# A vision-tower block on one core: the long convolution at its start, rebuilt in its tables, its products and its place beside the weight preparation

## The reference, cut to what matters

```python
dt = jnp.exp(log_dt)
A = -jnp.exp(inv_A_real) + 1j * A_imag
dtA = A * dt[:, None]
dA = (1.0 + dtA / 2) / (1.0 - dtA / 2)
V = jnp.exp(jnp.log(dA)[:, :, None] * jnp.arange(L))     # powers dA**l, l = 0 to 255
K = 2.0 * jnp.einsum('chn,hnl->chl', C * B[None], V).real # C is x
```

## Time and profile before

| what | value |
|---|---|
| median of 3 runs | 591.04 us (590.71 to 592.91) |
| profiled execution | 593.25 us, span 591.4 us |
| PE busy | 452.1 us, 76% |
| DVE busy | 379.4 us, 64% |
| ACT busy | 272.2 us, 46% |
| POOL busy | 188.3 us, 32% |
| mean granted clock of TensorE | 0.947 |
| powers, to the last square on DVE | 0 to 27.8 us |
| tables, to POOL's last | to 51.3 us |
| chunks, first product to last sum | 54.6 to 125.9 us |
| first statistics of a group | 133.5 us |

### The profile page before, as it was taken

One profiled execution on the slowest core, in us unless ns is written; L12 is line 12 of the kernel. 1 busy time (PEld: TensorE's weight loads), 2 busy tenths in 40 slices (PEclk: granted clock), 3 DMA queues, 4 the chain that ended last, 5 costly groups with the idle time before them and its releaser, 6 DMA issues. The chain is left out here.

```text
span 591.4 us, 11267 instructions
## 1 busy us (share of the span) xinstructions
PE 452.1 (76%) x3664; PEld 403.6 (68%) x3664; DVE 379.4 (64%) x895; ACT 272.2 (46%) x544; POOL 188.3 (32%) x156
## 2 busy tenths in 40 slices
PE   0000665584998999879999999998999999989645
PEld 0000654473776778668898898897988988989544
DVE  4999997766677665625466658557566485563632
ACT  1101342432776766454666545744565446544310
POOL 0197784722111210105070520703406107031200
PEclk9999999695999999969999999999999999999966
DMA  4100458953112202000010200201102001010101
GB/s 108 35 1 1 124 142 242 270 153 115 37 37 72 99 35 72 35 15 24 1 37 1 71 0 0 71 0 39 32 0 71 0 0 35 0 37 1 35 0 37
DMA packets 37816, 30.86 MB, mean 52 GB/s; under 512 B 19488, under 2 KB 31136, under 8 KB 37792
## 3 DMA queue, kind: packets, MB, share of 16 engines
q1 hardware_dynamic: 18848, 22.17, 12.1%
q10 hardware_dynamic: 18944, 8.39, 5.0%
HBM read 17.97 MB, written 12.58 MB: 52 GB/s over the span
## 5 line engine op out<-in xcount | busy, mean ns | idle before, releaser
L1109 PE MATMUL PS<-prods,Wa 128*64 128x64 f32 x512 | 37.7, 243 | 85.8 <-DVE prods L796 58.2
L978 DVE TENSOR_TENSOR gl<-PS,gh 128x512 fp32r<-128x512 f32 x64 | 44.2, 690 | 78.3 <-ACT gh L618 51.6
L1109 PEld LDWEIGHTS PS<-prods,Wa 128*64 128x64 f32 x512 | 32.2, 147 | 89.9 <-DVE prods L796 58.1
L615 ACT ACTIVATE PS<-PS,fc1bias 128x512 f32<-128x512 f32 x64 | 42.0, 657 | 94.8 <-PE PS L266 94.7
L264 PE MATMUL PS<-fc2h,gh 128*128 128x256 f32 x256 | 74.4, 291 | 6.0 <-DVE gl L978 5.2
L266 PE MATMUL PS<-fc2l,gh 128*128 128x256 f32 x256 | 72.3, 283 | 0.0
L265 PE MATMUL PS<-fc2h,gl 128*128 128x256 f32 x256 | 72.3, 282 | 0.0
L437 POOL TENSOR_SCALAR pst<-mv 128x4 f32<-128x4 f32 x16 | 3.6, 228 | 207.9 <-DVE pst L962 207.9
L264 PEld LDWEIGHTS PS<-fc2h,gh 128*128 128x128 f32 x256 | 48.6, 190 | 10.7 <-DVE gl L978 6.0
L264 PE MATMUL PS<-x2Th,fc1h 128*128 (+1 forms) x128 | 52.4, 409 | 2.1 <-DVE x2Tl L949 2.1
L265 PE MATMUL PS<-x2Th,fc1l 128*128 (+1 forms) x128 | 50.9, 398 | 0.0
(11 more groups left out here) (179 smaller groups left out, 1354.5 us busy)
## 6 DMA issues: line engine op xcount, KB each, us to landing
h_scratch<-tokev ACTq DMA_DIRECT2D x16, 256.0 KB, 3.0
h<-h_scratch SPq DMA_DIRECT2D x16, 256.0 KB, 5.0
q_scratch<-qe ACTq DMA_DIRECT2D x16, 256.0 KB, 2.1
qf<-q_scratch SPq DMA_DIRECT2D x16, 256.0 KB, 2.9
out_tokens<-outb SPq DMA_DIRECT2D x16, 256.0 KB, 2.2
...
craw<-in_c_ri SPq DMA_DIRECT2D x32, 64.0 KB, 2.4
...
```

The source lines that it names most:

```text
L615: act.activation(bank(j % 2), bank(j % 2), ACT.Gelu, bias=fc1bias[:, j:j + 1]).then_inc(gact, 1)
L978: dve.tensor_tensor(gl[:, j % 2, :], bank(j % 2), gh[:, j % 2, :].bitcast(F32), ALU.subtract).then_inc(gldone, 1)
L1109: mm = pe.matmul(dst, w[:, par, s * SUB + i, :, :].rearrange("p c d -> p (c d)"), prods[:, s, 0, i, :], start=x == 0, stop=x == 1)
```

## The change

It rebuilds the convolution in five places.

1. **Powers.** The squares move to ACT (`Square`). A level keeps two operations on DVE: the imaginary part, and the real part as twice the square of the real part minus the squared modulus; ACT squares the modulus as well. The three loads that the exponentials need go first, and ACT issues the two loads of `aim` itself. The first entries of `X` and `Y` are made by ACT too.
2. **Tables.** `Er`, `Ei` have seven entries (e = 1 to 7; EX). ACT copies entries 1, 2 and 4 of them; POOL makes entry 3, the third entry of `U`, and entries 5 to 7 in one rotation of three (18 operations after the powers). ACT makes the signed entries of `U`.
3. **Products.** A chunk is no longer cut in halves: DVE makes two products and a sum of 16 x 8 x 7 = 896 columns into `M`, which has a buffer for each parity; ACT copies `X` as the entry e = 0. PE runs all 32 matmuls of a chunk in one group, and ACT takes the result in one copy of 512 columns.
4. **Weights.** SP issues all weight loads right behind the first two chunks' c, and PE multiplies them before the token matmuls, while the tables are made. DVE's addition to `fc1bias`, which needs them, stands ahead of its first product.
5. **Loads of h0.** The first half goes out one or two loads at a time between the loads of c for chunks 12 to 15.

```diff
-SUB = 8
+EX = NE - 1
...
-            sp.dma_start(ldt[:, :], logdt.unsqueeze(0).to_broadcast([P, H])).then_inc(ld_tab, 16)
-            for r in range(2):
-                rows = slice(r * N, (r + 1) * N)
-                sp.dma_start(iar[rows, :], inv_ar).then_inc(ld_tab, 16)
-                sp.dma_start(aim[rows, :], a_im).then_inc(ld_tab, 16)
-                sp.dma_start(btab[rows, 0, :], b_ri[r]).then_inc(ld_tab, 16)
-                sp.dma_start(btab[rows, 1, :], b_ri[1 - r]).then_inc(ld_tab, 16)
+            halves = [slice(r * N, (r + 1) * N) for r in range(2)]
+            sp.dma_start(ldt[:, :], logdt.unsqueeze(0).to_broadcast([P, H])).then_inc(ld_exp, 16)
+            for rows in halves:
+                sp.dma_start(iar[rows, :], inv_ar).then_inc(ld_exp, 16)
+            for r, rows in enumerate(halves):
+                sp.dma_start(btab[rows, 0, :], b_ri[r]).then_inc(ld_b, 16)
+                sp.dma_start(btab[rows, 1, :], b_ri[1 - r]).then_inc(ld_b, 16)
...
-            with sp.Fori(0, PAIRS // 2 + 1) as it:
-                for par in range(2):
-                    load_c(it, par)
-            load_c(PAIRS // 2 + 1, 0)
-            load_h0(0)
-            load_c(PAIRS // 2 + 1, 1)
-            sp.wait_ge(dve_set, DVE_TABLES)
-            sp.wait_ge(pool_set, POOL_TABLES)
+            for par in range(2):
+                load_c(0, par)
+            sp.wait_ge(pool_set, 1)
             load_weight(routraw[:, :, 0:LEAVES - 1], routersT)
-            load_weight(wqraw[:, :, :], wq)
-            load_c(PAIRS // 2 + 2, 0)
-            load_weight(leafraw[:, :, :], leafT)
-            load_weight(woutraw[:, :, :], woutT)
-            load_c(PAIRS // 2 + 2, 1)
-            load_weight(fc1raw[:, :, :], fc1T)
-            load_c(PAIRS // 2 + 3, 0)
-            load_weight(projraw[:, :, :], projT)
-            load_c(PAIRS // 2 + 3, 1)
-            load_weight(fc2raw[:, :, :], fc2T)
-            load_h0(1)
+            for dst, src in ((wqraw, wq), (leafraw, leafT), (woutraw, woutT), (fc1raw, fc1T), (projraw, projT),
+                             (fc2raw, fc2T)):
+                load_weight(dst[:, :, :], src)
+            for n in range(2, CHUNKS - 5):
+                load_c(n // 2, n % 2)
+            load_c((CHUNKS - 5) // 2, (CHUNKS - 5) % 2)
+            for par in range(2):
+                sp.wait_ge(h0st[par], CREDIT + 16 * (PAIRS // 2))
+            load_h0(0, 0)
+            load_c((CHUNKS - 4) // 2, (CHUNKS - 4) % 2)
+            load_h0(0, 1)
+            load_h0(0, 2)
+            load_c((CHUNKS - 3) // 2, (CHUNKS - 3) % 2)
+            load_h0(0, 3)
+            load_h0(0, 4)
+            load_c((CHUNKS - 2) // 2, (CHUNKS - 2) % 2)
+            load_h0(0, 5)
+            load_h0(0, 6)
+            load_c((CHUNKS - 1) // 2, (CHUNKS - 1) % 2)
+            load_h0(0, 7)
+            for par in range(2):
+                sp.wait_ge(h0st[par], CREDIT + 16 * PAIRS)
+            for g in range(GROUPS):
+                load_h0(1, g)
...
-            link(pool.memset(Er[:, :, 0], 1.0))
-            link(pool.memset(Ei[:, :, 0], 0.0))
+            link(pool.memset(routraw[:, :, LEAVES - 1:LEAVES], 0.0))
+
+            def rotated(outr, outi, ar, ai, br, bi, t):
+                link(pool.tensor_tensor(outr, ar, br, ALU.mult))
+                link(pool.tensor_tensor(t, ai, bi, ALU.mult))
+                link(pool.tensor_tensor(outr, outr, t, ALU.subtract))
+                link(pool.tensor_tensor(outi, ar, bi, ALU.mult))
+                link(pool.tensor_tensor(t, ai, br, ALU.mult))
+                link(pool.tensor_tensor(outi, outi, t, ALU.add))
+
             pool.wait_ge(dve_set, DVE_POWERS)
...
+            rotated(Er[:, :, 2], Ei[:, :, 2], pw[:, 0, 0, :], pw[:, 0, 1, :], pw[:, 1, 0, :], pw[:, 1, 1, :],
+                    tE[:, :, 0])
+            rotated(U[:, 0, 2, :], ui[:, 2, :], U[:, 0, 0, :], ui[:, 0, :], U[:, 0, 1, :], ui[:, 1, :], tE[:, :, 0])
+            pool.wait_ge(e_out, 6)
+            wr, wi = (pw[:, 2, x, :].unsqueeze(2).to_broadcast([P, H, 3]) for x in range(2))
+            rotated(Er[:, :, 4:7], Ei[:, :, 4:7], Er[:, :, 0:3], Ei[:, :, 0:3], wr, wi, tE[:, :, :])
...
-            act.wait_ge(ld_tab, 16 * 9)
+            for r in range(2):
+                act.dma_start(aim[r * N:(r + 1) * N, :], a_im).then_inc(ld_aim, 16)
+            zi, omz, t0, den, m = (base[:, k, :] for k in (3, 4, 5, 6, 9))
+            act.wait_ge(ld_exp, 16 * 3)
             act.activation(base[:, 0, :], ldt[:, :], ACT.Exp).then_inc(act_tab, 1)
             act.activation(base[:, 1, :], iar[:, :], ACT.Exp).then_inc(act_tab, 1)
+            act.wait_ge(dve_set, 9)
+            act.activation(t0, zi, ACT.Square).then_inc(act_tab, 1)
+            act.wait_ge(dve_set, 10)
+            act.activation(den, omz, ACT.Square).then_inc(act_tab, 1)
+            act.wait_ge(ld_b, 16 * 4)
+            act.activation(X[:, :, 0], btab[:, 0, :], ACT.Copy, scale=sgn[:, 1:2]).then_inc(b_out, 1)
+            act.activation(Y[:, :, 0], btab[:, 1, :], ACT.Copy, scale=-2.0).then_inc(b_out, 1)
+            act.wait_ge(dve_set, DVE_Z)
+            act.activation(PS[:, 0, 0:H], pw[:, 0, 0, :], ACT.Square).then_inc(act_tab, 1)
+            act.activation(m, pw[:, 0, 1, :], ACT.Square).then_inc(act_tab, 1)
+            act.wait_ge(dve_set, DVE_Z + 3)
+            for j in range(1, LOGS - 1):
+                act.wait_ge(act_tab, 6 + 2 * (j - 1))
+                act.activation(base[:, 10 - j % 2, :], base[:, 9 + j % 2, :], ACT.Square).then_inc(act_tab, 1)
+                if j > 1:
+                    act.wait_ge(dve_set, DVE_Z + 3 + 2 * (j - 1))
+                act.activation(PS[:, 0, 0:H], power(j)[0], ACT.Square).then_inc(act_tab, 1)
 
             act.wait_ge(dve_set, DVE_POWERS)
             for j in range(3):
-                act.activation(PS[:, 5 + j, :], pwb[:, j, :, :].rearrange("p x h -> p (x h)"),
+                act.activation(bank((6, 7, 1)[j]), pwb[:, j, :, :].rearrange("p x h -> p (x h)"),
                                ACT.Copy).then_inc(pw_out, 1)
+            for e, j in ((0, 0), (1, 1), (3, 2)):
+                for x, t in enumerate((Er, Ei)):
+                    act.activation(t[:, :, e], pw[:, j, x, :], ACT.Copy).then_inc(e_out, 1)
+            for d in range(ND - 1):
+                if d == 2:
+                    act.wait_ge(pool_set, 1 + 2 * 6)
+                act.activation(U[:, 1, d, :], ui[:, d, :], ACT.Copy, scale=sgn[:, 0:1]).then_inc(u_out, 1)
 
             act.wait_ge(ld_qkv, 16)
             act.wait_ge(ld_const, 16 * 6)
...
                 n = 2 * it + par
-                act.wait_ge(vdone, CREDIT + 6 * (n - 1))
+                act.wait_ge(vdone, CREDIT + 3 * n - 4)
                 act.activation(bank(7 - par, D),
                                XY[:, bass.ds(n * CH, CH), :, :].rearrange("p h x a -> p (h x a)"),
                                ACT.Copy).then_inc(xyld, 1)
+                act.wait_ge(tokmm, CREDIT + n - 1)
+                apart(act)
+                act.activation(M[:, par, :, :, 0], X[:, bass.ds(n * CH, CH), :], ACT.Copy).then_inc(m0done, 1)
...
             def token_out(it, par):
                 n = 2 * it + par
                 act.wait_ge(h0st[par], CREDIT + 16 * it)
-                for s in range(2):
-                    act.wait_ge(tokmm, CREDIT + 2 * n + s + 1)
-                    act.activation(tokev[:, par, s * SUB // 2:(s + 1) * SUB // 2, :].rearrange("p g a -> p (g a)"),
-                                   bank(s, D), ACT.Copy).then_inc(tokout, 1)
+                act.wait_ge(tokmm, CREDIT + n + 1)
+                act.activation(tokev[:, par, :, :].rearrange("p g a -> p (g a)"), bank(par), ACT.Copy).then_inc(
+                    tokout, 1)
...
             act.wait_ge(dve_set, DVE_U)
+            act.wait_ge(pool_set, POOL_TABLES)
+            act.wait_ge(u_out, 3)
...
             link(dve.scalar_tensor_tensor(zr, ea, -0.5, dt, ALU.mult, ALU.mult))
+            dve.wait_ge(ld_aim, 16 * 2)
             link(dve.scalar_tensor_tensor(zi, aim[:, :], 0.5, dt, ALU.mult, ALU.mult))
             link(dve.tensor_scalar(omz, zr, -1.0, 1.0, ALU.mult, ALU.add))
-            tt(t0, zi, zi, ALU.mult)
-            tt(den, omz, omz, ALU.mult)
+            link(dve.scalar_tensor_tensor(nr, zr, 1.0, omz, ALU.add, ALU.mult))
+            dve.wait_ge(act_tab, 4)
             tt(den, den, t0, ALU.add)
+            tt(nr, nr, t0, ALU.subtract)
             link(dve.reciprocal(t1, den))
-            link(dve.scalar_tensor_tensor(nr, zr, 1.0, omz, ALU.add, ALU.mult))
-            tt(nr, nr, t0, ALU.subtract)
             tt(pw[:, 0, 0, :], nr, t1, ALU.mult)
             link(dve.scalar_tensor_tensor(pw[:, 0, 1, :], zi, 2.0, t1, ALU.mult, ALU.mult))
...
+            assert count[0] == DVE_Z, count[0]
+
+
+            link(dve.scalar_tensor_tensor(pw[:, 1, 1, :], pw[:, 0, 0, :], 2.0, pw[:, 0, 1, :], ALU.mult, ALU.mult))
+            dve.wait_ge(act_tab, 6)
```

(65 more changed lines are left out.)

140 lines of the change are left out of this document (45 added, 95 removed).

## The result

The changed kernel takes 581.73 us in the median (581.04 to 583.05) against 591.88 us (590.71 to 592.91) for the kernel before in the same comparison: a ratio of 0.983, 95% interval 0.980 to 0.986, so about 10 us less. That lies inside the range of 567 to 587 and 4.7 us above the 577 of the forecast. The profiled span is 581.3 us; the statistics of the first group, after which nothing is changed, start at 124.49 instead of 133.49. So 9.0 us come from ahead of them, and what lies behind them takes 456.8 us instead of 457.9.

A forecast was written before the change was run, and what follows sets the result against it. Powers, POOL's tables, then a two-chunk chain through ACT were taken to bound the time to the first group's statistics: 15.8 us earlier, less 1.5 for the clock, so 591.04 - 14.3 = 576.7, about 577 us; range 567 to 587.

The forecast's parts named there:

- powers: First stage, squares on ACT: 1.15 us a level, ended at 19.5 against 27.8, bounds 18.4 and 20.1.
- POOL's tables: Stage after the powers: three POOL rotations of 6.2, 6.2 and 10.9 us, ended at 42.9; first product at 44.2.
- two-chunk chain: Chunks: ACT's table copy for n+2 waits behind PE's chunk n; 8.12 us for two chunks, 4.06 each.
- hand-over: From DVE's last sum to the first group's statistics: 8.8 us, with statistics at 117.7 before the clock.
- the clock: PE in the chunks: gaps may bring half clock, up to 1.5 us a chunk; 1.5 us allowed in all.
- rival 1: Whole kernel as worked out: 577 us, own range 569 to 583; chance 0.70.
- statistics at 118 to 120: Sign: the first group's statistics on DVE start near 118 to 120 us, against 133.49 before.
- rival 3: PE stays at half clock through the chunks: two chunks take 9.6 us, total 585.5 us; chance 0.15.
- the first pair: Chunks 0 and 1: PE starts at half clock, 3.7 us instead of 2.2; chunk 2 starts at 53.8.
- The stall: DVE's 5.93 us standstill in the chunks: taken as 0 after the change, with 3 us as upper bound.
- DVE setting the pace: Rival for the chunks: ACT's order doesn't bind, 3.25 us a chunk, total 562.5 us; chance 0.11.
- rival 4: Slower: DVE loses time on rows of seven; 0.57 us more per instruction cancels the gain, up to 606.5 us; chance 0.04.

The follow-up runs named there:

- Kernel 6: Changed kernel with the seven levels of squares back on DVE, four operations each: 585.99 us, ratio 0.989.
- Kernel 1: Changed kernel with ACT's table copy of chunk n+2 moved ahead of the result copy of chunk n: 567.58 us, ratio 0.959.
- kernel 2: Changed kernel plus extra PE matmuls to keep the clock up, 12 after the weights and three ahead of each chunk's own: 576.18 us, ratio 0.973.
- Kernel 11: Kernel before the change with only its block of eight h0 loads spread out, weights left where they were: 587.34 us, ratio 0.993.
- kernels 4 and 5: Changed kernel: 4 loads and multiplies the weights after the tables, 583.00 us; 5 does so too and puts the eight h0 loads in one block, 585.66 us.
- kernels 9 and 10: On top of Kernel 1: 9 has late weights and the eight h0 loads in one block, 573.47 us; 10 has late weights alone, 570.91 us.
- kernel 10: Kernel 1 with the weights loaded and multiplied after the tables, h0 loads still spread: 570.91 us, ratio 0.964.

## Why the prediction was right, and where its sizes were off

The limits were the forecast ones: powers, then POOL's tables, then the two-chunk chain through ACT. That the total came within 4.7 us is partly luck. The chunks and the hand-over cost 8.6 us more than worked out before the clock (7.1 and 1.5), and only 1.5 were set aside for that. Tables 2.3 us earlier and 1.1 us less in the rest made up for a part. Of the bounds of rival 1, the tables (-1 to +3), the pace (3.9 to 4.3) and the clock (0 to 4) were all missed; and of the signs, two chunks per 8.1 us (9.1), no stall over 3 (3.40) and statistics at 118 to 120 (124.5) did not come. At 581.7 the result is nearer to rival 3's 585.5 than to 577.

**Powers: right, 0.7 us better.** Forecast end 19.5, measured 18.8, within the bounds 18.4 to 20.1. A level takes 0.95 instead of 1.15: the DVE step that reads PSUM takes 0.42, not the 0.60 of the tables' steps. Writing to PSUM is not the difference: two table steps that read PSUM and write SBUF took 1.26 together (20.21, `XY<-XY,PS`). What makes the tables' steps longer wasn't tested. In the powers no second table load follows the one at 1.97 (the next is for L659, in the MLP), so the 0 us for it was right. The Trainium skill, "ScalarE: Activation LUTs", section "Table sets: the hidden batching unit", warns of a reload where functions of two sets meet; 16 squares after two exponentials show no such load here. Kernel 6 puts the gain from the squares at 5.1 us at the first product.

**Tables: the right bound, 1.6 us better.** The rotations took 5.5, 4.9 and 11.0 us, against 6.2, 6.2 and 10.9; without the broadcast operand the products cost less, not as much as the sums. POOL's end, 40.5, lies below the stated bounds (41.8 to 44.9). First product at 41.87 instead of 44.2. The weight matmuls were hidden, done at 38.2 with 2.3 us to spare.

**The chain of two chunks: right.** Kernel 1 shows that ACT's order is the binding link, and kernel 2 that its length was nearly right: 4.13 a chunk against 4.06. Three instructions of 896 take 3.21 (3.17 forecast).

**The clock: the mis-sized term.** The text allowed 1.5 us, "since a delay of the second chunk of a pair evens out the gaps". It measured 7.2 us in the traces (kernel 2 against the changed kernel; 5.6 in the medians). The gaps did not even out: in most pairs DVE's two groups run back to back (51.94, 55.30), PE then has a gap of 2.6 to 4.1 us, and in six of seven cases the chunk after it runs partly or wholly at half clock (not the one at 64.03). Between chunk 2's product and the last sum's end this is 62.2 us instead of the forecast 55.1; 56.9 with the clock kept up, so 5.4 are the clock's and 1.8 are a chain a little longer than worked out. Another 1.6 us fall on the hand-over (10.3, and 8.7 in kernel 2), and 0.3 on the first pair. Rival 3, half clock throughout, priced the same mechanism with 10 us (585.5 - 577.0, and the 1.5 that the 577 holds); 7.2 lies nearer to it than to 1.5, and by the medians the measured price, 5.6, is halfway. The Trainium skill, "TensorE: Matmul & The Clock Gate", section "HAM oscillation — how this bites in real kernels", has a loop with a wait after every short burst, in which every burst starts at the low clock. The trace agrees in part: the chunks at 94.92 and 104.89 start at half clock behind gaps of 2.94 and 3.32 us, but the one at 55.20 starts at full clock behind 4.06. Here the bursts come from a pairing of chunks and not from a DMA.

The sum at the statistics: forecast 119.2 (117.7 and 1.5); -2.3 for the tables, +0.5 for the first pair, +7.1 for the chunks, +1.5 for the hand-over, -1.5 already allowed, gives 124.5, and 124.49 was measured. The rest of the program was 1.1 us shorter.

**The stall: right value, cause now known.** The stall of 5.9 that ended with a late load of c is gone, as taken; the wait of 3.40 at 101.63 ends with PE and belongs to the chain. The text gave two reasons, the weights gone and h0 spread. Kernel 11 shows that the block of eight h0 loads made nearly all of the stall, and kernels 4 and 5 that at the changed kernel's pace neither matters much. The edits pay where a chunk is quicker: the spread loads 4.3 us at 3.9 us a chunk (kernel 11) and 2.8 at 3.4 (kernels 9 and 10), the early weights 3.3 at 3.4 (kernel 10).

**Rivals.** DVE setting the pace was wrong for the change as made, and is what kernel 1 does up to its last chunks. Rows of seven cost nothing: 1.10 us for 896 columns against 1.23 for 1,024. (The 0.57 of rival 4 should read 0.59, 15.8 / 27; nothing hangs on it.)

What stays open: how to free the last chunks of kernel 1, which still lose 2 to 3 us, and its hand-over another 1.4 (10.2 against 8.8 forecast). There POOL waits 1.0 to 1.5 us for the load of c and PE up to 2.4 for POOL's product; a third buffer for c was not tried.
